# Retention block with a hash-routed mixture of experts: who turns the FFN input of batches 1 to 3, who adds the slots' biases, and where the next norm stands

## What is computed

```python
def ffn(x, ...):                       # x: layernorm(x1), 4096 tokens x 256
    shared = silu(x @ sw1 + sb1) * (x @ sw3 + sb3) @ sw2 + sb2      # 256 -> 512 -> 256
    for k in range(2):
        exp_ids = (tok * 11 + k * 7919) % 8                        # expert by token number
        h = gelu(x[of expert e] @ w1[e] + b1[e])                     # 256 -> 256
        y = h @ w2[e] + b2[e]
    return (shared + sum(y) / 2) / 2
x = x + attention(layernorm(x));  x = x + ffn(layernorm(x))
```

## Time and profile before

| | us |
|---|---|
| median of 3 runs (lowest to highest) | 443.07 (442.89 to 443.53) |
| the profiled execution itself | 443.2 |
| its span, first to last instruction | 441.4 |
| TensorE busy | 433.1 |
| VectorE busy | 292.7 |
| ScalarE busy | 216.3 |
| GpSimd busy | 95.6 |

### The profile page before, as it was taken

One profiled execution on the slowest core, in us unless ns is written; L12 is line 12 of the kernel. 1 busy time (PEld: TensorE's weight loads), 2 busy tenths in 40 slices (PEclk: granted clock), 3 DMA queues, 4 the chain that ended last, 5 costly groups with the idle time before them and its releaser, 6 DMA issues.

```text
span 441.4 us, 14549 instructions
## 1 busy us (share of the span) xinstructions
PE 433.1 (98%) x6318; PEld 391.6 (89%) x6318; DVE 292.7 (66%) x685; ACT 216.3 (49%) x416; POOL 95.6 (22%) x73
## 2 busy tenths in 40 slices
PE   6999999999999999999999999999999999999997
PEld 4999999999999999998989988899988999888995
DVE  6777778766886878967556654757538575475433
ACT  3456656546754477445255443472524823346430
POOL 1103223522254213640621101211004020040000
PEclk8999999999999999999999999999999999999999
DMA  7443332232321131226230005000133001120011
GB/s 260 146 148 99 99 99 76 75 94 80 126 95 51 51 124 54 91 79 222 94 115 1 26 25 208 31 0 0 48 122 116 0 0 48 48 95 0 1 48 48
DMA packets 15382, 34.64 MB, mean 78 GB/s; under 512 B 2368, under 2 KB 2656, under 8 KB 14816
## 3 DMA queue, kind: packets, MB, share of 16 engines
q1 hardware_dynamic: 14896, 33.05, 22.0%
q10 hardware_dynamic: 432, 0.79, 0.5%
HBM read 25.44 MB, written 8.40 MB: 77 GB/s over the span
## 4 chain that ended last, share of the span: by engine, by line
PE 91%; ACT 3%; DVE 3%; DMA 1%; issue 1%; POOL 0%; DVEq 0%; ACTq 0%
PE bank L358 50%; PE bank L367 13%; PE bank L368 7%; PE bank L437 5%; PE bank L480 4%; PE bank L467 3%; PE bank L451 2%; PE bank L563 2%; PE bank L416 1%; PE bank L377 1%; ACT kexp L681 1%; ACT vexp L681 1%; DMA xin<-xa 1%; PE bank L498 1%; DVE pm L873 1%
## 5 line engine op out<-in xcount | busy, mean ns | idle before, releaser
L778 ACT ACTIVATE xres<-bank,r1b 128x256 f32<-128x256 f32 x64 | 26.8, 470 | 54.9 <-PE bank L368 53.6
L358 PE MATMUL bank<-x2hi,sw_hi 128*128 128x512 f32 x128 | 51.3, 400 | 0.0
L763 ACT ACTIVATE sil<-bank,s1b 128x512 f32<-128x512 f32 x32 | 22.0, 688 | 58.4 <-PE bank L358 58.3
L358 PE MATMUL bank<-x2lo,sw_hi 128*128 128x512 f32 x128 | 50.4, 394 | 0.0
L358 PE MATMUL bank<-x2hi,sw_lo 128*128 128x512 f32 x128 | 50.3, 393 | 0.0
L696 ACT ACTIVATE keo<-kT,msk 128x512 f32<-128x512 f32 x32 | 21.4, 715 | 51.9 <-DVE kT L862 51.9
L367 PE MATMUL bank<-sw_both,ghi 128*128 128x512 f32 x128 | 46.5, 396 | 0.0
L367 PE MATMUL bank<-w_both,ehi 128*128 128x512 f32 x128 | 46.4, 397 | 0.0
L1045 DVE SCALAR_TENSOR_TENSOR gf<-bank,s3b,sil 128x512 f32<-128x512 f32 x32 | 23.9, 748 | 32.4 <-PE bank L358 32.4
L873 DVE TENSOR_TENSOR pm<-bank,msk 128x512 f32<-128x512 f32 x64 | 39.5, 679 | 2.3 <-PE bank L437 2.2
L358 PE MATMUL bank<-xhi,wqkv_hi 128*128 128x256 f32 x128 | 38.6, 302 | 0.9 <-DVE xlo L857 0.7
(11 more groups left out here) (119 smaller groups left out, 1133.7 us busy)
## 6 DMA issues: line engine op xcount, KB each, us to landing
xin<-xa SPq DMA_DIRECT2D x16, 256.0 KB, 3.3
w_raw<-w SPq DMA_DIRECT2D x16, 256.0 KB, 3.3
xres<-xs SPq DMA_DIRECT2D x16, 256.0 KB, 3.4
x_scratch<-xres SPq DMA_DIRECT2D x16, 256.0 KB, 3.4
xl<-x_scratch SPq DMA_DIRECT2D x8, 512.0 KB, 5.2
xr<-x_scratch SPq DMA_DIRECT2D x4, 1024.0 KB, 4.8
out<-xr SPq DMA_DIRECT2D x7, 512.0 KB, 2.6
sw_raw<-sw SPq DMA_DIRECT2D x6, 256.0 KB, 3.7
```

What stands on the lines that cost most here:

```text
L358: mm = nc.tensor.matmul(o, w[c][l], x[c][r], start=first and c == 0 and j == 0, stop=last and c == n - 1 and j == 2)
L763: nc.scalar.activation(sil[i % 2][:], h1_bank[i % 2][:], ACT.Silu, bias=s1b[:, m:m + 1]).then_inc(sil_ready, 1)
L778: ge = nc.scalar.activation(hf[q % 2][:, m, :], e_bank[q % 4][:, m * 2 * P:(m + 1) * 2 * P], ACT.Gelu, bias=r1b[:, e, m:m + 1])
```

## The change

For batches 1 to 3 the 16 transposes of TensorE are gone. VectorE turns the normed `xl` into a new SBUF tile `x2t` (8 KB a partition) by 32 `transpose` instructions a batch; each reads 32 partitions and writes 32 partitions, 256 elements on each, in squares of 32x32. They are spread over the experts' rounds as 2, 1, 2, 5, 5, 5, 5, 4 and 3. `high_x2` and `low_x2` read `x2t` in place of the PSUM banks. The norm of batch b+1 moves out of the rounds of b to stand beside the gates of b (its sums at i = 1 and 3, its apply at i = 2 and 4); for batch 1 it goes among batch 0's gates and residuals. The biases of the slots are added by VectorE in two halves at gates 5 and 6, in place of GpSimd's one operation. `low_expert` 7 moves ahead of `add_slot` 4. In the second half of the rounds `low_x2` is split around `add_slot` 6. ScalarE's wait for a slot moves from ahead of GELU to ahead of the copy that needs it. SP loads `xl` of batch b+2 between the two stores of batch b, once batch b+1 is turned, and batch 1's right after batch 0's transposes. The loops of SP and VectorE are written out; TensorE, ScalarE and GpSimd keep theirs.

```diff
+LN2_GATES, BIAS_GATES = (1, 2, 3, 4), (5, 6)
@@ SP
+            sp.wait_ge(t2_done, 4)
+            for half in range(2):
+                load_xl(1, half)
             for j in range(4):
                 store_x1(last, j)
             for j in range(4):
                 sp.wait_ge(x1_stored[j], NBATCH * 16)
-            with sp.Fori(0, last) as b:
-                sp.wait_ge(t2_done, (b + 1) * 4)
-                for half in range(2):
-                    load_xl(b + 1, half)
-                store(b, (4, 8))
+            for b in range(last):
+                store(b, 0, 4)
+                if b + 2 < NBATCH:
+                    sp.wait_ge(x2t_ready, (b + 1) * 2)
+                    for half in range(2):
+                        load_xl(b + 2, half)
+                store(b, 4, 8)
                 sp.wait_ge(stored, (b + 1) * 32)
                 sp.dma_start(xr[:], x1_dram[b + 1]).then_inc(xr_landed, 16)
@@ TensorE
-                slot(b, NE - 3)
-                if more:
-                    for j in range(4):
-                        transpose_x2(b + 1, j)
-                slot(b, NE - 2)
-                slot(b, NE - 1)
+                for i in range(NE - 3, NE):
+                    slot(b, i)
@@ ScalarE, high_x2 and experts
+                    act.wait_ge(x2t_ready, (b - 1) * 2 + (half + 1))
+                    src = x2t[:, c, half * HALF:(half + 1) * HALF]
...
                     if q >= 2:
                         act.wait_ge(elo_ready, b * NE + (q - 1))
-                    if q >= 4:
-                        act.wait_ge(slot_done, b * NE + (q - 2))
                     for m in range(MR):
                         ge = nc.scalar.activation(hf[q % 2][:, m, :], ...
                     act.wait_ge(gelu_ready, b * NE + (q + 1))
+                    if q >= 4:
+                        act.wait_ge(slot_done, b * NE + (q - 2))
                     nc.scalar.activation(ehi[expert_buffer(e)][:], hf[q % 2][:], ACT.Copy).then_inc(ehi_ready, 1)
@@ VectorE
+            def turn_x2(b, first, end):
+                for n in range(first, end):
+                    half, i, j = n // 16, n % 16 // 4, n % 4
+                    if n % 16 == 0:
+                        dve.wait_ge(xn2_ready, b * 2 + (half + 1))
+                    dst = x2t[32 * j:32 * j + 32, :, half * HALF:(half + 1) * HALF].rearrange("p c (t i k) -> p t c i k", i=4, k=32)
+                    src = xl[32 * i:32 * i + 32, 4 * half:4 * half + 4, :].rearrange("p t (c j k) -> p t c j k", c=CB, j=4)
+                    tr = nc.vector.transpose(dst[:, :, :, i, :], src[:, :, :, j, :])
+                    if n % 16 == 15:
+                        tr.then_inc(x2t_ready, 1)
...
             def experts(b, more):
+                runs = itertools.pairwise(itertools.accumulate((0, 2, 1, 2, 5, 5, 5, 5, 4, 3)))
+                def turn():
+                    if more:
+                        turn_x2(b + 1, *next(runs))
+                turn()
                 low_expert(b, 0)
+                turn()
                 low_expert(b, 1)
                 low_gate(b, 2 * MS - 1)
-                for q in range(2, NE):
-                    if more and q in (2, 4):
-                        ln2_sums(b + 1, q // 2 - 1)
+                turn()
+                low_expert(b, 2)
+                add_slot(b, 0)
+                for q in range(3, NE - 2):
                     low_expert(b, q)
-                    if more and q in (2, 4):
-                        ln2_apply(b + 1, q // 2 - 1)
+                    turn()
                     add_slot(b, q - 2)
+                low_expert(b, NE - 2)
+                turn()
+                low_expert(b, NE - 1)
+                add_slot(b, NE - 4)
+                turn()
+                add_slot(b, NE - 3)
                 if more:
-                    for j in range(4):
-                        low_x2(b + 1, j)
+                    low_x2(b + 1, 0)
+                    low_x2(b + 1, 1)
+                turn()
                 add_slot(b, NE - 2)
+                if more:
+                    low_x2(b + 1, 2)
+                    low_x2(b + 1, 3)
                 add_slot(b, NE - 1)
+            def beside_gates(b, i):
+                if 0 < b < last and i in LN2_GATES:
+                    n = LN2_GATES.index(i)
+                    (ln2_sums, ln2_apply)[n % 2](b + 1, n // 2)
+                if i in BIAS_GATES:
+                    n = BIAS_GATES.index(i)
+                    if n == 0:
+                        dve.wait_ge(xr_landed, (b + 1) * 16)
+                        dve.wait_ge(slots_landed, 64)
+                    at = slice(4 * n, 4 * n + 4)
+                    nc.vector.tensor_tensor(xr[:, at, :], xr[:, at, :], slot_bias[:, at, :], ALU.add).then_inc(biased, 1)
@@ VectorE, batch 0's shared stage
             low_gate(0, 2)
+            ln2_sums(1, 0)
             for j in range(4):
                 residual(last, j, last_out_bank[j])
+            ln2_apply(1, 0)
             for i in range(4, 8):
                 gate(0, i)
                 low_gate(0, i - 1)
-            with dve.Fori(0, last) as b:
+                if i == 4:
+                    ln2_sums(1, 1)
+                if i == 5:
+                    ln2_apply(1, 1)
+                beside_gates(0, i)
+            for b in range(last):
                 experts(b, True)
                 for i in range(2 * MS):
                     gate(b + 1, i)
                     if i:
                         low_gate(b + 1, i - 1)
+                    beside_gates(b + 1, i)
@@ GpSimd
-            def experts(b, more):
-                pool.wait_ge(xr_landed, (b + 1) * 16)
-                nc.gpsimd.tensor_tensor(xr[:], xr[:], slot_bias[:], ALU.add).then_inc(biased, 1)
-                if more:
-                    ln2_power(b + 1, 0)
-                    ln2_power(b + 1, 1)
...
-            pool.wait_ge(slots_landed, 64)
             with pool.Fori(0, last) as b:
-                experts(b, True)
-            experts(last, False)
+                ln2_power(b + 1, 0)
+                ln2_power(b + 1, 1)
```

More of the change, by code:

```diff
@@ L1 @@
+import itertools
 from contextlib import ExitStack
@@ L254, in load_slot_bias, with store @@
                 sp.dma_start(slot_bias[:, at, :], bias_dram[at].partition_broadcast(P)).then_inc(slots_landed, 16)
[L256 to L260, removed]
+            def store(b, first, end):
+                sp.wait_ge(o_ready, b * NE + end)
+                at = slice(first, end)
+                sp.dma_start(out[b].rearrange("p (s d) -> p s d", s=NE)[:, at, :], xr[:, at, :]).then_inc(stored, 16)
             def load_xl(b, half):
@@ L339, in _ @@
                 sp.wait_ge(x1_stored[j], NBATCH * 16)
-            with sp.Fori(0, last) as b:
-                sp.wait_ge(t2_done, (b + 1) * 4)
-                for half in range(2):
-                    load_xl(b + 1, half)
-                store(b, (4, 8))
+            for b in range(last):
[5 more added lines that the diff above has]
+                store(b, 4, 8)
                 sp.wait_ge(stored, (b + 1) * 32)
                 sp.dma_start(xr[:], x1_dram[b + 1]).then_inc(xr_landed, 16)
-            store(last, (4, 7, 8))
+            store(last, 0, 4)
+            store(last, 4, 7)
+            store(last, 7, 8)
             sp.wait_ge(stored, last * 32 + 48)
@@ L553, in step, with transpose_x2 @@
                     scores(h + 1)
-            def transpose_x2(b, j):
+            def transpose_x2(j):
                 half, c = j // CB, j % CB
-                if j == 0 and not (isinstance(b, int) and b == 0):
-                    pe.wait_ge(gelu_ready, b * NE)
                 if c == 0:
-                    pe.wait_ge(xn2_ready, b * 2 + (half + 1))
+                    pe.wait_ge(xn2_ready, half + 1)
                 for t in range(4):
@@ L609, in slot, with experts @@
                 wide_product(o_bank[s % 2][:], g, w).then_inc(slot_done, 1)
-            def experts(b, more):
+            def experts(b):
                 for q in range(3):
@@ L662, in _ @@
             with pe.Fori(0, last) as b:
-                experts(b, True)
+                experts(b)
                 for i in range(2 * MS):
                     shared(b + 1, i)
-            experts(last, False)
+            experts(last)
         @block.scalar
@@ L751, in high_x2 @@
                 half, c = j // CB, j % CB
-                act.wait_ge(t2_done, b * 4 + (j + 1))
-                cp = nc.scalar.activation(x2hi[:, c, half * HALF:(half + 1) * HALF], t2_bank[j][:], ACT.Copy)
+                if isinstance(b, int) and b == 0:
+                    act.wait_ge(t2_done, j + 1)
+                    src = t2_bank[j][:]
+                else:
+                    act.wait_ge(x2t_ready, (b - 1) * 2 + (half + 1))
+                    src = x2t[:, c, half * HALF:(half + 1) * HALF]
+                cp = nc.scalar.activation(x2hi[:, c, half * HALF:(half + 1) * HALF], src, ACT.Copy)
                 if half == 0:
```

(8 more changed lines are left out.)

13 lines of the change are left out of this document (7 added, 6 removed).

## The result

The changed kernel takes 437.39 us (436.86 to 437.68) against 443.53 beside it, a ratio of 0.986 (95%: 0.9844 to 0.9875), 6.1 us less. Forecast were 437.8 us and a range of 437.0 to 441.5. The 443.53 is a new measurement of the kernel before; the forecast started from 443.07.

What follows compares the result with a forecast made beforehand. TensorE, busy without a gap, was taken as the bound; removing its transposes, 3 x 1.75 = 5.25 us, with VectorE's added work hidden, took 443.2 to 437.95, or 437.8 us against the median; range 437.0 to 441.5.

Steps and rivals of the forecast that it cites:

- The term of TensorE: Between slots 5 and 6, 16 transposes leave TensorE's queue: 1.75 us, three times in the kernel, 5.25 us in all.
- Turns at 0.45, biases at 1.14 us: VectorE's new work: 32 transposes a batch at 0.45 us each, and two bias additions at 1.14 us each.
- the 48 to 50 named as a sign: VectorE busy 48 to 50 us in each batch period would show the forecast right.
- The timetable: When VectorE's gates, low parts, turns and adds finish against TensorE's need: no waits, or a tenth or two in batch 0.
- the gap between sums and apply: In the norm, apply starts 3.67 us after the sums because GpSimd's power lies between.
- The spares before slots 6 and 7: At the end of the rounds, adds 4 and 5 finish 0.7 and 0.9 us before TensorE needs them.
- The reload of xr: Follows the second store, issued 3.7 us into the shared stage, landed 4.9 us later; first bias 19.4 us into it.
- Rival 1, small waits: VectorE is up to a microsecond late at its narrow places: 437.9 to 441.5 us; chance 0.14.
- the place named: Batch 0's gate 7 and le1, the tightest place: spares of 0.5 and 0.15 us before expert 2 and slot 0.
- Rivals 2 and 3: In the rounds, turns at 0.69 us eat the gain (443.4 us, chance 0.05); over 0.72 us, slower (chance 0.11).
- frees some 4 us of VectorE a batch: Without GpSimd's 4.63 us bias addition, a VectorE subtraction is no longer held for 4.70 us instead of 0.68.

Runs made afterwards that it cites:

- few turns: Changed kernel with only 2 of the 32 turns made in each of batches 2 and 3, batch 1 making all: 437.36 us, ratio 0.9867.
- 2 more turns: Changed kernel with 2 more turns, into unused memory, in each of the four runs of five turns a batch: 437.23 us.
- 3 more a run: Changed kernel with 3 more turns, into unused memory, in each of the four runs of five turns a batch: 440.78 us, ratio 0.9941.
- The written-out loops: Kernel before with only the loops of SP and VectorE written out, as the change has them: 442.95 us, ratio 1.000.

## Why the prediction was right

- **The term of TensorE**: 5.25 forecast, 5.22 between fixed points of the two profiles, 5.21 lost again when only the turning is undone.
- **Turns at 0.45, biases at 1.14 us**: 0.45 and 1.14. Their bounds (0.33 to 0.69, 1.14 to 2.3) were not needed. VectorE's 47.4 us a period were given as 48.5, and lie just under the 48 to 50 named as a sign.
- **The timetable**: gate 7 was put at 22.97 us into the period (288.58 for a period from 265.61), late by VectorE's backlog. It starts at 22.49 (285.73, period from 263.24) and waits 0.23 us for TensorE: no backlog is left. The step that was too careful is the gap between sums and apply, 3.67 us in the text and 3.30 here (270.15 to 273.45): GpSimd's power takes 1.01 us where the earlier trace rows had 1.42, and a gate and a low part fill the gap. The spares before slots 6 and 7 were given as 0.7 and 0.9 and are 0.57 and 0.67: the joints between unlike operations cost some 0.1 us more than from the earlier trace rows.
- **The reload of xr**: put at 3.7 us into the shared stage "as before". It is issued 6.1 us into it (269.37), since the second store now waits for add_slot 7 behind two low parts and lands later. The first bias, 18.65 us into the stage (281.89), did not feel it; GpSimd's biases did.
- **Rival 1, small waits**: not in the forecast execution, but real: 0.65 us once, in the place named. Two other slow profiled executions, 438.79 (few turns) and 438.62 (2 more turns), are slow by their start: their last scores begin at 191.22 and 191.05.
- **Rivals 2 and 3**: their premise (0.69 us a turn) is false; their price was tested by added turns. With 3 more a run, VectorE was late as described, at 1.1 us a batch. Its turns cost as if 0.65 us each, and the prediction's own prices, 1.9 us a batch at 0.69 and 1.9 to 2.4 less for every 0.1 us below, give 0.9 to 1.1 there. The point at which lateness begins to cost lies between 0.58 and 0.65.
- **What the sum did not hold**: the gain was 6.1 us and not 5.25. The 437.8 came this close in part by luck: from the 443.53 measured beside the changed kernel the same sum gives 438.3. In the profiles the extra is 0.62 us at the start, and its cause is open (last section).

The step most at risk was one the prediction passed in a clause: that the biases' move "frees some 4 us of VectorE a batch". Undone, it costs 6 to 13 us.

## What to carry to other kernels

When one engine is busy without a gap, price what leaves its queue from the chain's start times, and spend the effort on a timetable of the engine that takes the work: which instruction is due when, and what stands ahead of it. An average load of 47 us in 56 says too little: with the same load, the norm in its old place made the kernel 5.5 us slower than the kernel before. And move long GpSimd operations away from dense VectorE stretches before filling these.

## What was not expected of the hardware

**The clock can fall after a wait.** In the run with GpSimd's biases ahead of the powers, TensorE waits 3.04 us at 341.3; the stretches around it, with the granted clock as third last number, and the first matmuls behind it:

```profile
340.00:343.00 3.00, 1.32 (x6) 0.74 (x4) 0.74 (x3) 0.00 (x0) 2.23 (x2) 1.00 0.00 0
343.00:346.00 3.00, 1.64 (x4) 1.35 (x5) 3.00 (x8) 1.21 (x2) 0.00 (x0) 0.65 0.00 0
```

```profile
344.36 0.80 PE L371 MATMUL bank<-x2hi,sw_hi 128*128 128x512 f32 x1 [3.04 <-DVE gf L1069]
344.95 0.63 PE L371 MATMUL bank<-x2hi,sw_lo 128*128 128x512 f32 x1
```

The matmuls soon follow each other by 0.43 us (the third starts at 345.38) instead of 0.233: the lower level, 1.2 GHz. A wait is then dearer than its length. After the wait of 3.24 us at 280.9 in the same execution the clock stayed up, so it is not certain either; the five other runs of this kernel were granted 0.988 to 0.992 on average and took 1.4 to 2.6 us more than the profiled one (0.996). So the clock bears part of the gap between 5.8 and 13 us: some 0.6 us in the profiled execution, and how much in the others was not measured by itself.

**A slow pace at the start.** The first products of the kernel before, then of the changed one:

```profile
10.56 0.41 PE L358 MATMUL bank<-xlo,wqkv_hi 128*128 128x256 f32 x1
10.78 0.41 PE L358 MATMUL bank<-xhi,wqkv_hi 128*128 128x256 f32 x1
```

```profile
9.69 0.28 PE L371 MATMUL bank<-xlo,wqkv_hi 128*128 128x256 f32 x1
9.81 0.28 PE L371 MATMUL bank<-xhi,wqkv_hi 128*128 128x256 f32 x1
```

0.22 against 0.12 us apart. Between 9 and 11 us the granted clock was 0.50 in the first, the 1.2 GHz level, and 1.00 in the second; TensorE had waited 1.97 us for the first x in one and 1.29 in the other. Neither the wait nor the granted clock settles it, as the run with only the turning undone shows:

```profile
7.28 1.09 PE L390 MATMUL bank<-msk,xin 128*128 128x128 f32 x4 [0.67 <-DVE xin L866]
...
10.38 0.41 PE L371 MATMUL bank<-xlo,wqkv_hi 128*128 128x256 f32 x1
10.59 0.41 PE L371 MATMUL bank<-xhi,wqkv_hi 128*128 128x256 f32 x1
```

Here the products follow each other by 0.21 us after a wait of 0.67 us, and the record gives a granted clock of 1.00. The written-out loops (1.00 us of wait) and the 2 more turns (0.98) show the same, while profiles with waits of 0.92 to 1.50 us have 0.12. So in three of five slow starts the granted clock does not show why.

Both paces occur in either kernel: with the slow one the last scores begin at 190.4 to 191.2 us, with the fast one at 189.4 to 189.9.

**How often it starts late is open.** The changed kernel and its variants without a wait gained more than 5.25 us in every comparison: 6.1, 5.8 (few turns), 5.9 (2 more turns) and 5.75. If each execution takes 243.0 or 248.2 us from the last scores to the last addition, and 4.6 us of its time lie outside, as in the profiled ones, then by an estimate from the totals the last scores began later than 190.1 us in 57 of 97 executions with TensorE's transposes and in 3 of 18 without. That is hardly chance. It is not the written-out loops, nor anything that the run with only the turning undone keeps, since both behave like the kernel before. What in the turning moves the start, or whether the stretch behind the last scores differs in executions that were not profiled, no run shows.
